# A gated-delta-rule layer with experts on Trainium2: inverting the 32x32 blocks by rows on 128 partitions, with VectorE making the turned blocks

## The reference

```python
mixed = jax.nn.silu(_causal_conv1d(hidden_states @ w_qkv, conv_w))      # q, k, v
z = (hidden_states @ w_z).reshape(Bb, Ss, HV, DV)
beta = jax.nn.sigmoid(b)
g = -jnp.exp(A_log) * jax.nn.softplus(a + dt_bias)

def step(St, inp):                       # scan over the 256 tokens
    q_t, k_t, v_t, g_t, b_t = inp
    St = St * jnp.exp(g_t)[..., None, None]
    v_old = jnp.einsum('bhk,bhkv->bhv', k_t, St)
    delta = (v_t - v_old) * b_t[..., None]
    St = St + k_t[..., None] * delta[:, :, None, :]
    o = jnp.einsum('bhk,bhkv->bhv', q_t, St)
    return (St, o)

core = core * jax.lax.rsqrt(var + EPS) * norm_weight * jax.nn.silu(z)
return core.reshape(Bb, Ss, VDIM) @ w_out
```

## Time and profile before

| | before |
|---|---|
| median of 3 runs | 1287.56 us (1286.76 to 1291.09) |
| the profiled execution | 1299.38 us |
| its span | 1297.6 us |
| TensorE busy | 1114.2 us, 86% |
| VectorE busy | 840.6 us, 65% |
| ScalarE busy | 648.8 us, 50% |
| GpSimd busy | 653.1 us, 50% |
| mean granted TensorE clock | 0.93 |

### The profile page before, as it was taken

One profiled execution on the slowest core, in us unless ns is written; L12 is line 12 of the kernel. 1 busy time (PEld: TensorE's weight loads), 2 busy tenths in 40 slices (PEclk: granted clock), 3 DMA queues, 4 the chain that ended last, 5 costly groups with the idle time before them and its releaser, 6 DMA issues.

```text
span 1297.6 us, 22128 instructions
## 1 busy us (share of the span) xinstructions
PE 1114.2 (86%) x8190; PEld 840.1 (65%) x8190; DVE 840.6 (65%) x1469; ACT 648.8 (50%) x1192; POOL 653.1 (50%) x1076
## 2 busy tenths in 40 slices
PE   4899999855898989899799979897998999698747
PEld 3676666523576776768486757676775768486636
DVE  5532222278776788587959776886879497758304
ACT  3321222144574657376556747573756476466412
POOL 2601000158384838574774758385838555682720
PEclk8989999987897999899989989997999899899959
...
GB/s 326 319 96 24 42 45 21 94 103 68 67 59 100 37 127 8 128 32 103 35 99 36 98 84 50 101 33 102 53 113 24 110 32 103 45 64 42 19 31 41
DMA packets 140761, 101.06 MB, mean 78 GB/s; under 512 B 113904, under 2 KB 127856, under 8 KB 137328
## 3 DMA queue, kind: packets, MB, share of 16 engines
...
q0 software_dynamic: 1536, 4.20, 0.9%
...
## 4 chain that ended last, share of the span: by engine, by line
PE 50%; DVE 23%; issue 5%; ACT 2%; DVEq 0%
DVE conv L1104 7%; DVE nm L1141 7%; PE rv L1369 6%; PE pj L1236 5%; PE ra L1336 5%; PE pj L1237 4%; PE pj L1238 4%; PE rv L1352 4%; DVE eg L1113 4%; PE ra L1326 3%; PE ra L1319 3%; PE rv L1344 2%; PE rv L1353 2%; PE pk L1277 2%; DVE acc L1210 2%
## 5 line engine op out<-in xcount | busy, mean ns | idle before, releaser
L1104 DVE SCALAR_TENSOR_TENSOR conv<-pj,taps,conv 128x510 f32<-128x510 f32 (+2 forms) x384 | 285.2, 744 | 93.3 <-ACT conv L997 82.8
L960 POOL TENSOR_TENSOR halves<-halves 64x30 f32<-64x30 f32 (+14 forms) x480 | 262.8, 547 | 37.6
L957 POOL TENSOR_TENSOR halves<-halves 64x30 f32<-64x30 f32 (+14 forms) x480 | 249.8, 520 | 37.6
L1236 PE MATMUL pj<-xhi,whi 128*128 128x512 f32 x384 | 184.1, 479 | 58.5 <-DVE conv L1104 55.4
L1238 PE MATMUL pj<-xhi,wlo 128*128 128x512 f32 x384 | 158.7, 413 | 0.0
L1237 PE MATMUL pj<-xlo,whi 128*128 128x512 f32 x384 | 158.6, 413 | 0.0
L1369 PE MATMUL rv<-wo,gated 128*128 128x256 f32 x512 | 152.7, 427 | 1.7 <-DVE acc L1210 1.4
L1141 DVE SCALAR_TENSOR_TENSOR nm<-pk,wneg,eg 128x512 f32<-128x512 f32 (+1 forms) x256 | 139.5, 606 | 14.5 <-PE pk L1280 14.4
L1236 PEld LDWEIGHTS pj<-xhi,whi 128*128 128x128 f32 x384 | 76.2, 198 | 111.7 <-DVE conv L1104 67.4
L997 ACT ACTIVATE conv<-pj,taps 128x512 f32<-128x512 f32 x128 | 87.6, 685 | 108.4 <-PE pj L1238 107.6
L951 POOL MEMSET halves<- 64x32 f32 x16 | 2.4, 152 | 273.0 <-DMA halves<-n_scratch 273.0
...
## 6 DMA issues: line engine op xcount, KB each, us to landing
...
halves<-n_scratch SPq DMA_DIRECT2D x32, 128.0 KB, 2.5
r_scratch<-halves SPq DMA_DIRECT2D x32, 128.0 KB
```

Source lines behind the costliest of these rows:

```text
L957: gp.tensor_tensor(tmp, rb[:, 0:t, t:t + 1].to_broadcast([4 * NM, t, w]), rb[:, t:t + 1, t + 1:].to_broadcast([4 * NM, t, w]), ALU.mult).t ...
L960: gp.tensor_tensor(rb[:, 0:t, t + 1:], rb[:, 0:t, t + 1:], tmp, ALU.add).then_inc(elim, 1)
L1104: v.scalar_tensor_tensor(out=y, in0=it.pbank[item][:, :, 0:S - s], scalar=taps[par][:, piece(j)[0], KS - 1 - s:KS - s], in1=y, op0=ALU.mul ...
L1236: te.matmul(bank, whi[par][w], xhi[:, k, cols], start=(k == 0), stop=False)
```

## The change

- GpSimd's elimination works **on all 128 partitions**. Each block is loaded twice, into partitions 0 to 63 and 64 to 127 (`halves[0]`, two DMAs of 64 partitions). The inverse is built in a new tile `rows`: partitions 0 to 63 hold its even rows and 64 to 127 its odd rows, 16 rows of 32 each. For t from 0 to 30 the multiply and the add work on t//2+1 rows of 31-t values. That is 62 instructions instead of 60, each on up to 136 values of a partition where it was up to 240. Three memsets ahead of the wait for the blocks put ones and zeros into `rows`.
- GpSimd's **turned copy** (L963) is gone, and with it the turned blocks' way to DRAM (L893) and back (L903).
- **VectorE** makes the turned blocks out of `rf` with three 32x32-block transposes, in a new item LA1 in its order. It waits there for all of `blocks_back`. TensorE's LA1 waits for two of them, its LB1 for the third.
- `blocks_out` writes only the two diagonal parts of a matrix, in eight DMAs instead of four. `blocks_back` is one DMA out and eight in, instead of four out and seven in.
- The three orders change around it. On VectorE D3 goes ahead of P4, LA1 comes between P6 and OUT3, and P7 goes behind OUT4. On TensorE OUT6 goes ahead of P1 and OUT7 behind U1_0. ScalarE's order of SO, E0, E1, W and P1 changes.

```diff
-    n_dram = nc.dram_tensor("n_scratch", (4, REP * B * 3, C32, C32), F32).ap()
-    r_dram = nc.dram_tensor("r_scratch", (4, 2 * REP * B, C32, C32), F32).ap()
-    rt_dram = nc.dram_tensor("rt_scratch", (4, 2 * REP * B, C32, C32), F32).ap()
+    n_dram = nc.dram_tensor("n_scratch", (4, 2, REP * B, C32, C32), F32).ap()
+    r_dram = nc.dram_tensor("r_scratch", (2, 4, 2 * REP * B, C32 // 2, C32), F32).ap()
...
+            HR = C32 // 2
+            rows = sb("rows", [P, HR * C32 + 136], F32, c3)
+            nb = halves[0][:].rearrange("p (i c) -> p i c", c=C32)
+            rb = rows[:, 0:HR * C32].rearrange("p (i c) -> p i c", c=C32)
+            prod = rows[:, HR * C32:]
...
-            ORDER_V = ("D0 SO D1 SQ K0 D2 K1 OUT0 P4 OUT1 D3 P5 K2 OUT2 P6 OUT3 P7 K3 OUT4 P0 OUT5 OUT6 OUT7 P1 N21_0 N21_1 P2 O0 O1 "
-                       "P3 O2 O3").split()
+            ORDER_V = ("D0 SO D1 SQ K0 D2 K1 OUT0 D3 P4 OUT1 P5 K2 OUT2 P6 LA1 OUT3 K3 OUT4 P7 P0 OUT5 OUT6 P1 OUT7 N21_0 N21_1 P2 O0 "
+                       "O1 P3 O2 O3").split()
...
-                    for c in range(2):
-                        sp.dma_start(rb[2 * NM * c:2 * NM * (c + 1)],
-                                     n_dram.rearrange("q (m k) i x -> k q m (i x)", k=3)[c]).then_inc(rb_in, 16)
+                        for k in range(2):
+                            sp.dma_start(n_dram[q, k].rearrange("m i x -> i m x"), cols[:, k, :, first:first + C32]
+                                         ).then_inc(blocks_out_sem, 16)
+                    at_least(sp, blocks_out_sem, 128, n, 128)
+                    for h in range(2):
+                        sp.dma_start(halves[0][C64 * h:C64 * (h + 1)],
+                                     n_dram.rearrange("q k m i x -> (q k m) (i x)")).then_inc(rb_in, 16)
...
+                    sp.dma_start(r_dram.rearrange("h q m i x -> (h q m) (i x)"), rows[:, 0:HR * C32]).then_inc(r_out, 16)
+                    sp.wait_ge(r_out, 16 * n + 16)
                     at_least(sp, a_full, 1, it.a_before("U2_1"), 0)
+                    for q in (0, 2, 1, 3):
+                        for h in range(2):
+                            sp.dma_start(rf[C32 * q + h:C32 * (q + 1):2, :, C32 * q:C32 * (q + 1)],
+                                         r_dram[h, q].rearrange("m i x -> i m x")).then_inc(back_in, 16)
...
+                    gp.memset(rows[:, 0:HR * C32], 0.0).then_inc(elim, 1)
+                    gp.wait_ge(elim, first + 1)
+                    for h in range(2):
+                        gp.memset(rows[C64 * h:C64 * (h + 1), h:HR * C32:C32 + 2], 1.0).then_inc(elim, 1)
+                    count = 3
+                    gp.wait_ge(rb_in, 32 * n + 32)
+                    for t in range(C32 - 1):
+                        w, r = C32 - 1 - t, t // 2 + 1
+                        tmp = prod[:, 0:r * w].rearrange("p (i c) -> p i c", c=w)
+                        gp.wait_ge(elim, first + count)
+                        gp.tensor_tensor(tmp, rb[:, 0:r, t:t + 1].to_broadcast([P, r, w]),
+                                         nb[:, t:t + 1, t + 1:].to_broadcast([P, r, w]), ALU.mult).then_inc(elim, 1)
+                        gp.wait_ge(elim, first + count + 1)
+                        gp.tensor_tensor(rb[:, 0:r, t + 1:], rb[:, 0:r, t + 1:], tmp, ALU.add).then_inc(elim, 1)
                         count += 2
-                    gp.wait_ge(elim, n * NELIM + count)
-                    gp.tensor_copy(rbt, rb.rearrange("p i c -> p c i")).then_inc(elim, 1)
...
+                        elif item == "LA1":
+                            v.wait_ge(back_in, 128 * b + 128)
+                            v.transpose(t64[0:C32, :, 0:C32], rf[0:C32, :, 0:C32]).then_inc(tt_made, 1)
+                            v.transpose(tc2[C64:C64 + C32], rf[C64:C64 + C32, :, C64:C64 + C32]).then_inc(tt_made, 1)
+                            v.transpose(t64[C32:C64, :, C32:C64], rf[C32:C64, :, C32:C64]).then_inc(tt_made, 1)
...
-                            te.wait_ge(turned_in, 48 * b + 48)
+                            te.wait_ge(tt_made, 3 * b + 2)
```

More of the change, by code:

```diff
@@ L729, in build @@
             out_sem = sem("out_written", c3)
-            NELIM = 2 * (C32 - 2) + 2
-            ORDER = ("Z0 SO Z1 SQ Z2 K0 Z3 K1 P4 OUT0 K2 P5 OUT1 P6 OUT2 P7 OUT3 K3 LA1 OUT4 LA2 P0 OUT5 P1 LB1_0 LB1_1 LB2_0 OUT6 "
-                     "LB2_1 OUT7 P2 U1_0 U1_1 N21_0 N21_1 U2_0 U2_1 VT0 O0 P3 O1 VT1 O2 VT2 O3 VT3").split()
-            ORDER_A = ("SQ Z0 Z1 E0 E1 SO Z2 Z3 P4 W P5 SK S4 E2 S5 P6 P7 E3 LA1 S6 LA2 P0 S7 LB1_0 LB1_1 LB2_0 P1 LB2_1 S0 U1_0 U1_1 "
+            NELIM = 2 * (C32 - 1) + 3
+            ORDER = ("Z0 SO Z1 SQ Z2 K0 Z3 K1 P4 OUT0 K2 P5 OUT1 P6 OUT2 P7 OUT3 K3 LA1 OUT4 LA2 P0 OUT5 OUT6 P1 LB1_0 LB1_1 LB2_0 "
+                     "LB2_1 P2 U1_0 OUT7 U1_1 N21_0 N21_1 U2_0 U2_1 VT0 O0 P3 O1 VT1 O2 VT2 O3 VT3").split()
+            ORDER_A = ("Z0 SQ Z1 SO E0 E1 Z2 W Z3 P4 P5 SK S4 E2 S5 P6 P7 E3 LA1 S6 LA2 P0 S7 LB1_0 LB1_1 P1 S0 LB2_0 LB2_1 U1_0 U1_1 "
                        "S1 U2_0 U2_1 P2 VT0 O0 P3 O1 S2 VT1 O2 VT2 O3 S3 VT3").split()
-            ORDER_V = ("D0 SO D1 SQ K0 D2 K1 OUT0 P4 OUT1 D3 P5 K2 OUT2 P6 OUT3 P7 K3 OUT4 P0 OUT5 OUT6 OUT7 P1 N21_0 N21_1 P2 O0 O1 "
-                       "P3 O2 O3").split()
+            ORDER_V = ("D0 SO D1 SQ K0 D2 K1 OUT0 D3 P4 OUT1 P5 K2 OUT2 P6 LA1 OUT3 K3 OUT4 P7 P0 OUT5 OUT6 P1 OUT7 N21_0 N21_1 P2 O0 "
+                       "O1 P3 O2 O3").split()
             RING_A = {"LA1": 1, "LA2": 1, "LB1": 2, "LB2": 2, "U1": 2, "U2": 2, "VT": 4}
@@ L874, in blocks_out @@
                         first = C32 * q
[L875 to L882 removed]
+                        cols = nm[par][first:first + C32].rearrange("p m w e -> p (m w e)").rearrange("p (m k s) -> p k m s", k=3, s=S)
+                        for k in range(2):
[5 more added lines that the diff above has]
+                                     n_dram.rearrange("q k m i x -> (q k m) (i x)")).then_inc(rb_in, 16)
                 def blocks_back(n, it):
@@ L944, in eliminate @@
                 def eliminate(n, it):
-                    gp.wait_ge(rb_in, 32 * n + 32)
                     if "W" in it.items:
                         gp.wait_ge(head_w_lo, 2 * n + 4)
-                    at_least(gp, rt_out, 32, n, 0)
-                    gp.memset(rb.rearrange("p i c -> p (i c)")[:, 0:C32 * C32:C32 + 1], 1.0).then_inc(elim, 1)
-                    count = 1
-                    for t in range(C32 - 2, 0, -1):
-                        w = C32 - 1 - t
-                        tmp = prod[:, 0:t * w].rearrange("p (i c) -> p i c", c=w)
-                        gp.wait_ge(elim, n * NELIM + count)
-                        gp.tensor_tensor(tmp, rb[:, 0:t, t:t + 1].to_broadcast([4 * NM, t, w]),
-                                         rb[:, t:t + 1, t + 1:].to_broadcast([4 * NM, t, w]), ALU.mult).then_inc(elim, 1)
-                        gp.wait_ge(elim, n * NELIM + count + 1)
-                        gp.tensor_tensor(rb[:, 0:t, t + 1:], rb[:, 0:t, t + 1:], tmp, ALU.add).then_inc(elim, 1)
+                    at_least(gp, elim, NELIM, n, 0)
+                    at_least(gp, r_out, 16, n, 0)
+                    first = n * NELIM
+                    gp.memset(rows[:, 0:HR * C32], 0.0).then_inc(elim, 1)
[12 more added lines that the diff above has]
+                        gp.tensor_tensor(rb[:, 0:r, t + 1:], rb[:, 0:r, t + 1:], tmp, ALU.add).then_inc(elim, 1)
                         count += 2
-                    gp.wait_ge(elim, n * NELIM + count)
-                    gp.tensor_copy(rbt, rb.rearrange("p i c -> p c i")).then_inc(elim, 1)
                 gp.memset(rf[:], 0.0).then_inc(init, 1)
@@ L1316, in run @@
                             i = number(item)
+                            te.wait_ge(tt_made, 3 * b + 3)
                             bank = fill_a(it, item, "LA2")
```

28 lines of the change are left out of this document (2 added, 26 removed).

## The result

The changed kernel takes 1284.84 us (median of 20 runs, 1277.75 to 1289.93); the kernel before, beside it on the same chip, 1289.66 (20 runs). The ratio is 0.9961, with a 95% interval of 0.9944 to 0.9977: 5 us faster. 34 were forecast, and the time lies above the range.

What follows compares the result with a forecast made beforehand. It took TensorE to nearly bind short rounds and the 55.1 us chain through GpSimd to lengthen the others. Thirteen rounds falling from 60.85 to 58.3 us, head 0 +2.8, the end −3.9: −34 us, 1253 us, range 1224 to 1282.

Steps and rivals of the forecast that it cites:

- What bounds the kernel: Rounds alternate 54.7 and 65.1 us: TensorE nearly binds the short; a 6.41 us LA1 wait and its clock lengthen the other.
- The new chain: From K3 through GpSimd's elimination and DMAs: blocks back after 47.7 us, with ends from 36 to 62.
- The fit from two sizes of instruction: GpSimd's elimination: multiply and add times at two sizes give 387 and 396 ns, 29.1 us with gaps.
- Where the chain meets the round: At VectorE's LA1: blocks come 5 us before VectorE needs them in a 58 us round; alternation ends.
- the forecast's formula: VectorE reaches LA1 T − 5.2 us after the last K3, T being the round; blocks are back after 47.7.
- The new wait: TensorE waits 2.8 us (2.4 to 4.2) at LA1 for two VectorE transposes every round; 57.5 us at full clock.
- the replay: The short round of before retimed with the new order: LA1 waits 2.8 us; chance of 1240 to 1267 us 0.50.
- The clock: TensorE's clock behind the LA1 wait: half of a 1.7 us loss, 0.8 us a round, making T 58.3.
- The sum: Thirteen rounds −33 us, head 0 +2.8, head 15 at the end −3.9: −34 us, 1253 us.
- the clock gives it back: Rival: TensorE's clock falls to 0.51 over 10 us every round, 62.4 us a round, 1312 us; chance of slower 0.11.

Runs made afterwards that it cites:

- run 8: The changed kernel with VectorE's transposes ahead of P6 and D3 back behind P4 and OUT1: 0.9632 of the kernel before, 1255.78 us.
- Run 10: The changed kernel with D3 back behind P4 and OUT1 and six surplus TensorE multiplications covering LA1's wait: 0.9626 of the kernel before, 1240.42 us.
- Run 3: The changed kernel with fourteen surplus GpSimd multiplications ahead of each elimination, lengthening the chain: 1.0209 of the kernel before, 1315.49 us.
- Run 9: The changed kernel with only D3's scans moved back behind P4 and OUT1 on VectorE: 0.9968 of the kernel before, 1285.00 us.
- run 6: The new elimination and transposes with the three old orders of the kernel before: 1.0031 of the kernel before, 1307.89 us.
- run 7: The old elimination, transfers and turned copy with the three new orders of the change: 0.9914 of the kernel before, 1292.35 us.
- run 11: The changed kernel with GpSimd's subtraction wlo cut into twelve instructions, D3 still ahead of P4: 0.982 of the kernel before, 1264.57 us.

## Why the prediction was wrong

By its own steps:

- **What bounds the kernel.** Right: the long rounds of before are a wait and its clock, and the alternation went with the long chain.
- **The new chain**, 47.7 us to the blocks and 49.1 to LA1. Right: 46.2 and 47.7 at the last head, each part within 1 us or so. The fit from two sizes of instruction gave the elimination to 3%.
- **Where the chain meets the round.** Right: no wait of VectorE, in rounds of 57.5 us (runs 8, 10) either. Run 3 gives a slack of 6.4 us, where the forecast's formula has 8 or more at that length of round.
- **The new wait**, 2.8 us, and a round of 57.5 us at full clock. Right in size: 2.80 where nothing is held, and 57.5 in runs 8 and 10, 58.1 to 58.5 in the change. "D3 ahead of P4 moves P6's projection, but P7 waits for P5 as before" looked at TensorE only. What D3 meets on GpSimd at its new place wasn't asked, though the trace of before held the collision in two rounds. The waits ahead of P6 and P7 came to 2.7 us a round, where the replay kept 2.0.
- **The clock**, 0.8 us a round. **This step failed.** It measured 3.9. The two rows of before, a 2.01 us wait without loss and a 2.71 us wait with 1.7, were taken as the price of "a wait of this size" and halved. Run 9 shows the price of the new wait with the scans out of the way: 5.1 us of loss in eleven of thirteen rounds, 3.4 in the other two, and a round of 61.4 us instead of 57.5, so 3.9 in time. Run 10 takes only that away and gains 44.6 us. Thirteen rounds times 3.1 us (3.9 − 0.8) are 40 us; the rounds missed the forecast by 37 to 41 (a gain of 33 forecast, a loss of 4 to 8 measured).
- **The sum.** The end makes up for part of it, −10.9 in place of −3.9. Of these 7 us 4.9 lie behind the last LA1, where the clock comes back sooner with the new orders (runs 6 and 7), which the sum left out. The +2.8 for head 0 didn't show: from its first projection to the thirteen rounds it is 123.5 us after the change and 124.9 and 124.3 before. That the time came within 3 us of the range's upper end is therefore partly luck.

So the mechanism of the rival "the clock gives it back" happened, near its turning point: it was priced at 4.9 us a round and to decide from 3.3. The rounds did get longer, and only the end kept the kernel from being slower. The rival was given little weight because rows 10 showed a smaller loss behind a single wait. The trace of before had nearer evidence. In its rounds of 64 to 68 us TensorE waits some 2 us ahead of P7 and then again at LA1, the pair that the new order makes in every round; in one of them the second wait was 3.49 us, hardly more than the 2.8 of the forecast:

```profile
395.33 0.50 PE L1236 MATMUL pj<-xhi,whi 128*128 128x512 f32 x1 [1.95 <-DVE conv L1104]
...
404.31 0.23 PE L1298 MATMUL ra<-halves,nm 32*32 32x32 f32 x1 [3.49 <-DVE nm L1141]
```

```profile
403.30:413.60 10.30, 9.29 (x173) 7.61 (x174) 3.40 (x7) 4.14 (x8) 0.00 (x0) 0.50 0.39 67
```

The clock was at half for 10.2 us behind it, as behind 6.41 us. And the price in time stood in rows 1 and 2: 65.1 − 54.7 − 6.41 = 4.0 us for these 10 us at half clock, not up to 4.9. With 57.5 + 4.0 = 61.5 us for a round the forecast would have met run 9's 61.4 and the change's 61.2.

**Open.** The same waits don't always cost the same: with 2.8 us at LA1 in every round, run 9 has no round at full clock and run 11 has five. The round from 549.7 us of the change has LA1's 2.8 us and 2.4 us ahead of P, and a clock of 1.00 throughout; the round from 732.8 has 2.8 and 1.9, and loses 5.1 us. What sets the difference between such rounds no run here shows, nor how much the faster elimination is worth under the orders of runs 8 and 10: the old one wasn't tried there.
